# Third group's base blocks moved ahead of its last unit, half of the first two groups' blocks drained by ScalarE with x added by transfers

## The reference, cut to what matters

```python
ek = exp(min(k, 30)); ekv = ek * v                       # here k = v = fside, r = x
nf, df = forward scan of (ekv, ek) over T with a decay per channel and batch
nb, db = the same scan backward
euk = exp(min(u + k, 30))
y = sigmoid(x) * (nf + nb - ekv + euk * v) / max(df + db - ek + euk, 1e-8) * (0.8 + 0.2 * tf)
h = silu(y @ rw1.T + rb1)                                # 64 wide
logits = (h @ rw2.T + rb2)[:, :16] + gates               # the top 2 of 16, softmax: coeff
base = y @ W.T + bias                                    # 1024 x 1024
xa = y @ A.T                                             # 16 experts of rank 16
out = x + base + (xa * coeff) @ B
```

## Time and profile before

| What | Value |
|---|---|
| median of 3 runs | 682.68 us (680.84 to 684.97) |
| profiled execution | 681.2 us |
| span of its trace (first to last instruction) | 679.3 us |
| granted TensorE clock, mean over the span | 0.962 of full |
| TensorE matmul busy | 591.5 us (87%) |
| VectorE busy | 517.9 us (76%) |
| ScalarE busy | 360.0 us (53%) |
| GpSimd busy | 369.0 us (54%) |

### The profile page before, as it was taken

One profiled execution on the slowest core, in us unless ns is written; L12 is line 12 of the kernel. 1 busy time (PEld: TensorE's weight loads), 2 busy tenths in 40 slices (PEclk: granted clock), 3 DMA queues, 4 the chain that ended last, 5 costly groups with the idle time before them and its releaser, 6 DMA issues.

```text
span 679.3 us, 6881 instructions
## 1 busy us (share of the span) xinstructions
PE 591.5 (87%) x2546; PEld 477.2 (70%) x2546; DVE 517.9 (76%) x578; ACT 360.0 (53%) x428; POOL 369.0 (54%) x183
## 2 busy tenths in 40 slices
PE   0143698979999849699999999999999999999997
PEld 0132476758878627588888887888788887888886
DVE  7999999999999997999789996999699322021202
ACT  5778898855745665747635574567455221011100
POOL 1899998868768872856535854485457401000100
PEclk9976799989999968989999999999999999999999
DMA  5334477526747711244413442336222502040112
GB/s 194 123 93 151 147 237 239 169 65 140 175 120 140 201 63 62 78 141 159 151 47 108 154 157 77 109 109 202 77 84 73 154 1 74 20 154 2 30 63 78
DMA packets 33249, 78.45 MB, mean 115 GB/s; under 512 B 4736, under 2 KB 4928, under 8 KB 33216
## 3 DMA queue, kind: packets, MB, share of 16 engines
q1 hardware_dynamic: 30912, 73.82, 33.1%
q0 software_dynamic: 2304, 4.20, 4.2%
HBM read 57.03 MB, written 20.97 MB: 115 GB/s over the span
## 4 chain that ended last, share of the span: by engine, by line
PE 73%; DVE 13%; POOL 6%; ACT 4%; issue 3%; DMA 1%; SPq 0%; POOLq 0%; DVEq 0%; ACTq 0%
PE acc L940 23%; PE acc L942 22%; PE acc L941 22%; DVE mix L739 2%; PE acc L951 2%; DVE mix L730 2%; DVE mix L734 2%; PE acc L952 2%; DVE mix L760 2%; DVE eu L749 1%; PE acc L989 1%; DVE yr L766 1%; DMA xo<-w_base 1%; POOL wx_lo L652 1%; DVE kv L744 1%
## 5 line engine op out<-in xcount | busy, mean ns | idle before, releaser
L940 PE MATMUL acc<-y_hi,wa_hi 128*128 128x512 f32 x640 | 258.7, 404 | 61.9 <-POOL y_lo L639 51.0
L941 PE MATMUL acc<-y_lo,wa_hi 128*128 128x512 f32 x640 | 255.0, 398 | 0.0
L942 PE MATMUL acc<-y_hi,wa_lo 128*128 128x512 f32 x640 | 254.8, 398 | 0.0
L940 PEld LDWEIGHTS acc<-y_hi,wa_hi 128*128 128x128 f32 x640 | 123.7, 193 | 94.3 <-POOL y_lo L639 52.3
L942 PEld LDWEIGHTS acc<-y_hi,wa_lo 128*128 128x128 f32 x640 | 123.4, 193 | 26.7
L941 PEld LDWEIGHTS acc<-y_lo,wa_hi 128*128 128x128 f32 x640 | 123.7, 193 | 25.2
L629 POOL TENSOR_TENSOR mix<-mix,kv 128x1024 f32<-128x1024 f32 x31 | 74.3, 2396 | 88.6 <-DVE mix L718 88.6
L773 DVE SCALAR_TENSOR_TENSOR xo<-acc,bias_sb,xo 128x512 f32<-128x512 f32 x64 | 46.7, 736 | 74.3 <-PE acc L942 73.0
L639 POOL TENSOR_TENSOR y_lo<-yr,y_hi 128x1024 fp32r<-128x1024 f32 x31 | 75.8, 2445 | 36.0 <-ACT y_hi L401 36.0
L652 POOL TENSOR_TENSOR wx_lo<-xa,wx_hi 128x512 fp32r<-128x512 f32 x16 | 20.8, 1322 | 115.0 <-ACT wx_hi L478 115.0
L604 POOL TENSOR_TENSOR mix<-mix,kv 128x1024 f32<-128x1024 f32 x31 | 74.2, 2394 | 8.8 <-DVE mix L760 8.8
(11 more groups left out here) (103 smaller groups left out, 695.0 us busy)
## 6 DMA issues: line engine op xcount, KB each, us to landing
kv<-f_cm SPq DMA_DIRECT2D x32, 512.0 KB, 3.4
yr<-x_cm SPq DMA_DIRECT2D x32, 512.0 KB, 3.4
out<-xo SPq DMA_DIRECT2D x64, 256.0 KB, 3.3
xo<-x_cm SPq DMA_DIRECT2D x64, 256.0 KB, 3.7
out<-xo POOLq DMA_DIRECT2D x16, 256.0 KB, 6.5
xa<-w_base SPq DMA_DIRECT2D x5, 512.0 KB, 3.6
xo<-w_base SPq DMA_DIRECT2D x3, 512.0 KB, 5.9
xo<-w_router_a SPq DMA_DIRECT2D x2, 480.0 KB, 3.4
```

The costliest lines, as they stand in the source:

```text
L940: nc.tensor.matmul(out_ap, wh, yh, start=start, stop=False)
L941: nc.tensor.matmul(out_ap, wh, yl, start=False, stop=False)
L942: return nc.tensor.matmul(out_ap, wl, yh, start=False, stop=stop)
```

## The change

Five things are done in one edit.

1. Blocks j = 4 to 7 of groups 0 and 1 (8 of the 16) are no longer evacuated by VectorE. ScalarE does `drain`: it adds the bias and writes the block to an `xo` slot; no x is loaded for them. Four transfers issued by GpSimd (`add_x`, one for each j = 4 to 7, 128 channels by 1024 time steps, from `x_cm` to `out`) add x. `drain(e)` waits until the slot's last `add_out` has landed.
2. Group 2 on TensorE: `hid_sum` (three matmuls into 64 rows) takes the place of `hid`; base blocks 0 and 1 for units 0 to 6 are made before the last unit; `last_unit` takes the last unit's high half before its low half; base block 2 for units 0 to 6 stands before `turn`. ScalarE makes the sigmoid directly from the sum (`sigmoid_sum`), without `low_rows` and `hidden`.
3. Unit 15: `inverse` and `ratio` are made in two halves, the later half in time first (`ratio_late`). Unit 16's `p1` moves from GpSimd to VectorE.
4. Group 3's routing stands one step earlier (`first_step(3)` is 19 for 20), with base block 2 for three units before `turn` and three behind it; group 4 makes base block 0 for its first five units before it asks for the last three.
5. Places of evacuations, adds, x loads and routing pieces in the steps of groups 0 to 4 are moved, by tables.

```diff
-        evacs_at = {(CB + 2, AFTER_FWD): (0, 2), (CB + 2, AFTER_FWD_NUM): (2, 4), (CB + 2, AFTER_BWD_DEN): (4, 5),
+        evacs_at = {(CB + 2, AFTER_FWD): (0, 2), (CB + 2, AFTER_FWD_NUM): (2, 4), (CB + 5, AFTER_FWD_NUM): (8, 9),
+                    (CB + 5, AFTER_BWD_DEN): (9, 11), (CB + 5, AFTER_SUM): (11, 12),
...
+        drains_at = {(CB + 2, AFTER_INVERSE): (4, 6), (CB + 3, AFTER_HI): (6, 7), (CB + 3, AFTER_EXP_K): (7, 8),
+                     (CB + 5, AFTER_EXP_K): (12, 13), (CB + 5, AFTER_INVERSE): (13, 14), (CB + 6, AFTER_HI): (14, 15),
+                     (CB + 6, AFTER_EXP_K): (15, 16)}
+        x_adds_at = {(CB, AFTER_LO): (4, 5), (CB + 1, AFTER_GATE): (5, 7), (CB + 1, AFTER_LO): (7, 8)}
         adds_at = {(CB + 2, AFTER_LO): (0, 3), (CB + 3, AFTER_GATE): (3, 6), (CB + 4, AFTER_GATE): (6, 8),
-                   (CB + 5, AFTER_GATE): (8, 10), (CB + 5, AFTER_LO): (10, 13), (CB + 6, AFTER_GATE): (13, 16)}
+                   (CB + 6, AFTER_GATE): (8, 11), (CB + 6, AFTER_LO): (11, 14), (CB + 7, AFTER_GATE): (14, 16)}
...
+            def drain(e):
+                G, j = divmod(e, CB)
+                act.wait_ge(out_done, e + 1)
+                if e < XBUF:
+                    act.wait_ge(part_stored[(e - 2) % PBUF], 16 * (PARTS // PBUF))
+                else:
+                    act.wait_ge(out_added[e % XBUF], 16 * (e // XBUF))
+                nc.scalar.activation(xo[:, e % XBUF, :], acc[:, out_bank(G, j), :], ACT.Identity,
+                                     bias=bias_sb[:, j:j + 1]).then_inc(drained, 1)
...
+            def add_x(j):
+                pool.wait_ge(part_stored[j % PBUF], 16 * ((j + CB) // PBUF + 1))
+                nc.gpsimd.dma_start(out[j], x_cm[j], accum_op=ALU.add,
+                                    max_dma_last_dim=4 * T).then_inc(x_added[j - CB // 2], 16)
...
                 if g in HALVED:
                     nc.vector.tensor_tensor_scan(a[:, T - 2:N - 1:-1], decay(g, N - 1), a[:, T - 2:N - 1:-1], a[:, T - 1:T],
                                                  ALU.mult, ALU.add).then_inc(late_num_bwd, 1)
+                    ratio_late(g)
...
+            def last_unit(G, kc):
...
+                pe.wait_ge(late_hi_ready, 1)
+                nc.tensor.matmul(sums, wr[:, kc, 0:HID], yh, start=False, stop=False)
+                nc.tensor.matmul(sums, wr[:, kc, HID:2 * HID], yh, start=False, stop=False)
+                for a in range(2):
+                    nc.tensor.matmul(ranks[a], wa_hi[:, kc, cols[a]], yh, start=False, stop=False)
+                    nc.tensor.matmul(ranks[a], wa_lo[:, kc, cols[a]], yh, start=False, stop=False)
+                pe.wait_ge(late_lo_ready, 1)
+                nc.tensor.matmul(sums, wr[:, kc, 0:HID], yl, start=False, stop=True).then_inc(hid_done, 1)
...
+                elif G == SPLIT:
+                    bank_in(G, 0)
+                    made = 0
+                    for kc in range(CB - 1):
+                        while made < (kc if kc == CB - 2 else kc - LAG + 1):
+                            if made == 0:
+                                bank_in(G, 4)
+                            for j in range(2):
+                                base(G, j, made)
+                            made += 1
+                        unit_in(G, kc)
+                        hid_sum(G, kc)
...
+                    last_unit(G, CB - 1)
...
-                ahead = 4 if G == SPLIT else 0
+                ahead = {0: CB, SPLIT: CB - 1, 3: 3}.get(G, k0)
```

More of the change, by code:

```diff
@@ L211, in decay_mix_with_routed_lora_channel_major @@
         part_out = sem("part_out")
+        x_added = [sem(f"x_added{j}") for j in range(CB // 2)]
+        drained = sem("drained")
         out_added = [sem(f"out_added{i}") for i in range(XBUF)]
@@ L339, in _ @@
                 ended = ends_at.get(s, -1)
+                if 1 <= s < UNITS - 1 and ended in (SPLIT, SPLIT + 1):
+                    load_k(s + 1)
                 if ended >= 0:
@@ L344, in _ @@
                     store(G * CB)
-                if 1 <= s < UNITS - 1:
+                if 1 <= s < UNITS - 1 and ended not in (SPLIT, SPLIT + 1):
                     load_k(s + 1)
@@ L373, in _ @@
                     load_x(e)
+            for j in range(CB // 2):
+                sp.wait_ge(x_added[j], 16)
             for i in range(XBUF):
@@ L505, in _ @@
                 late_split, late_sigmoid = held(s - 1), held(s - 2)
-                third = s == first_step(SPLIT)
-                if q == 1 and G != SPLIT:
+                if s == THIRD:
+                    split_late_hi(s - 1)
+                    sigmoid_r(s)
+                    scale_end_den(s)
+                    sigmoid_sum(SPLIT)
+                    copy_xa(SPLIT)
+                    exps()
+                    split_hi(s - 1)
+                    scale_end_num(s)
+                    exp_gap(SPLIT)
+                    exp_uk(s)
+                    exp_k(s + 1)
+                    copy_turned(SPLIT)
+                    split_wx(SPLIT)
+                    inverse(s)
+                    continue
+                routed = q == 1 and G != SPLIT
+                if routed:
                     sigmoid_z(G)
@@ L561, in _ @@
                     exps()
[L562 removed]
+                if q == 0:
                     low_rows(G)
@@ L567, in _ @@
                     inverse(s)
-                if third:
-                    copy_turned(G)
+                drains(s, AFTER_INVERSE)
+                if routed and G == 1:
+                    split_wx(G)
                 for n in chunks_at(hi_steps, s):
@@ L678, in _ @@
                     split_lo(s - 1)
-                if q == 1 and G == SPLIT:
-                    split_wx(G)
+                if s == THIRD:
+                    split_wx(SPLIT)
+                for j in tiles(x_adds_at, s, AFTER_GATE):
+                    add_x(j)
                 for e in tiles(adds_at, s, AFTER_GATE):
@@ L856, in _, with groups_at @@
             link(nc.vector.tensor_copy(d_ps[:, 0:UNITS], d_g[:, :, :].rearrange("p b c -> p (b c)")))
-            def first_groups(s, place):
+            def groups_at(s, place):
                 for e in tiles(evacs_at, s, place):
                     evacuate(*divmod(e, CB))
+                if (s, place) in hidden_at:
+                    hidden(hidden_at[s, place])
+                if (s, place) in silu_at:
+                    silu(silu_at[s, place])
+                if (s, place) in routing_at:
+                    routing(routing_at[s, place])
+                if (s, place) in weigh_at:
+                    weigh(weigh_at[s, place])
             for s in range(STEPS):
                 G, q = quarter(s)
-                stored = q == 2 and G >= SPLIT
+                stored = q == 2 and G > 4
                 ended = ends_at.get(s, -1)
-                ending = ended >= 0
+                ending = ended > 4
                 if ending:
@@ L946, in y_of, with hid_sum @@
                 return y_hi[:, s, :], y_lo[:, s, :]
+            def hid_sum(G, kc):
+                yh, yl = y_of(G, kc)
+                three(acc[0:HID, banks[G][0], :], wr[:, kc, 0:HID], wr[:, kc, HID:2 * HID], yh, yl, kc == 0, False)
+            def last_unit(G, kc):
+                yh, yl = y_of(G, kc)
+                cols = [slice(a * P, (a + 1) * P) for a in range(2)]
+                sums = acc[0:HID, banks[G][0], :]
+                ranks = [acc[:, banks[G][1 + a], :] for a in range(2)]
+                pe.wait_ge(late_hi_ready, 1)
[6 more added lines that the diff above has]
+                nc.tensor.matmul(sums, wr[:, kc, 0:HID], yl, start=False, stop=True).then_inc(hid_done, 1)
+                for a in range(2):
+                    nc.tensor.matmul(ranks[a], wa_hi[:, kc, cols[a]], yl, start=False, stop=True).then_inc(xa_done, 1)
             def hid(G, kc):
@@ L1067, in _ @@
                             low_rank(G, a, kc)
+                    if G == 4:
+                        bank_in(G, 3)
+                        for kc in range(first):
+                            base(G, 0, kc)
                     for kc in range(first, CB):
@@ L1117, in _ @@
                 for j in range(3, 5):
-                    for kc in range(k0 + 2, k0 + 4):
+                    for kc in range(k0 + first, k0 + 4):
                         base(G, j, kc)
```

265 lines of the change are left out of this document (147 added, 118 removed).

## The result

The changed kernel takes 674.5 us (median of 4 runs, 673.5 to 675.1) against 682.4 us before (median of 4): ratio 0.9884, 95% interval 0.9858 to 0.9911, so 7.9 us are won. The forecast was 672.0, a gain of some 10. The profiled execution has a span of 672.4 us, 6.9 less than before.

What follows compares the result with a forecast made beforehand. TensorE's waits and low clock between 222.40 and 288.83, some 25 us, were the bound, with VectorE setting the time until unit 15. 18.4 won less 8.2 in group 4 is 10.2; 682.68 becomes 672.5, stated 672.0, range 664 to 680.

Steps and rivals of the forecast that it cites:

- the likeliest case: The forecast itself, rated against its rivals: 18.4 us won less 8.2 given back, time 669 to 675, chance 0.45.
- forward(13) waits for p1(13): VectorE, step 13: forward(13) can begin at 203.0 instead of 205.68, 2.7 won, with some 4 us of VectorE idle.
- at 222.4 again: TensorE: the order of groups 0 and 1 hardly changes, so group 2 begins at 222.4 as before.
- The drain waits for a landing: ScalarE near 224: drain of e = 14 waits 4 to 6 us for add_out(8), issued at 222.4, landing at 228.4.
- give nothing at this point: VectorE up to ratio(14): relief by ScalarE wins nothing, as 4 us won are lost waiting for a transfer.
- rival B: Adds land early enough or drain 14's wait hides; TensorE never waits for unit 15's high half: 665 to 669, chance 0.20.
- TensorE at unit 15: Group 2: TensorE waits 2.9 us for the high half at 249.1; group 3 begins at 300.8, 18.4 won.
- Group 4: TensorE waits 5.8 us for unit 23 and loses 2.4 in clock: 8.2 given back, 10.2 left.
- From `ratio(23)` to its low half are 8.5: Unit 23, asked for in group 4: low half ready 8.5 us after ratio(23), at z + 90.6, z being group 3's start.
- Each us there is one us at the end.: VectorE's steps 20 to 23: each us longer or shorter than counted moves the end by one us.
- Rival F: Slow x transfers delay add_out(0), so drain(6), ScalarE and VectorE wait: 20 slower, 700; decides from about 14 each; chance 0.06.
- between 2.33, after which the clock stayed up, and 3.64, after which it fell: TensorE, group 2: the 2.9 us wait lies between these; clock taken as up, 2 us kept for the other case.

Runs made afterwards that it cites:

- experiment 4: Changed kernel with weigh(3) behind three VectorE operations, the inverse of unit 20 ahead of the wx split on ScalarE, p1(21) ahead of it on GpSimd: 668.9 us, ratio 0.9804.
- experiment 5: Changed kernel with four edits together: early adds, load of r(24) ahead of two stores, p1(13) and p1(21) ahead of wx_lo, late weigh(3): 666.3 us, ratio 0.9768.
- experiment 6: Changed kernel with only two edits: p1 ahead of the low halves of wx in groups 1 and 3, and late weigh(3): 666.6 us, ratio 0.9769.
- experiment 11: Kernel with all four edits, plus five more base blocks moved ahead in group 4 and scale_end_den(12) ahead of the xa copies on ScalarE: 665.1 us, ratio 0.9738.
- Experiment 7: Changed kernel with part one undone: all 16 evacuations of groups 0 and 1 on VectorE, no ScalarE drains, no x adds in memory: 675.9 us, ratio 0.9905.
- Experiment 1: Changed kernel with the adds of e = 8 to 10 issued a step earlier, at the end of GpSimd's step 13: 671.9 us, ratio 0.9861.
- experiment 8: Changed kernel with TensorE's group 2 order undone for base block 1, its seven blocks again behind the last unit: 678.3 us, ratio 0.9940.
- Experiment 2: Changed kernel with the load of r(24) issued ahead of the stores of e = 30 and 31 in SP's queue: 673.0 us, ratio 0.9866.
- Experiment 9: Changed kernel with group 4's five advanced base blocks put back behind its last three units: 677.3 us, ratio 0.9926.
- experiment 12: Changed kernel without the four transfers that add x in main memory: 674.4 us, ratio 0.9885.

## Why the prediction was right, and where it was off

The time (674.5) lies in the likeliest case (669 to 675), 2.5 above the 672.0 named, and the mechanism is the forecast one: won in group 2, part given back in group 4, none lost later. Its steps:

- **forward(13) waits for p1(13).** Right in kind and size: 3.89 us for "some 4". Its time was wrong, 205.28 for 203.0. The step by which `weigh` still waits for TensorE, whose `spread` stands where it stood, so that `wx_lo` is ready when it was, failed: `routing(1)` stands behind `p2(12)` now, TensorE waits 2.40 for its result, and `wx_lo` starts at 200.35 instead of 197.91. From the logits of group 1 to its first weighted half TensorE needs 17.75 us, where it needed 13.61: 4.1 lost, 2.4 in this wait and some 1.6 in eight matmuls at the half clock behind it. So it begins group 2 at 224.85 and not "at 222.4 again"; the prediction had put this term at nothing. Where the clock stayed up behind the same wait (experiments 4, 5 and 6) it is 16.7. This was not undone alone; experiment 11, next to it, could not settle its worth.
- **The drain waits for a landing.** Right, but 2.90 us and not 4 to 6: the adds were issued at 224.80 (expected 222.4) and the first was there after 4.0, where 6.0 was taken. Two errors cancel by luck, and `ratio(14)` is at 235.06 for 234.5. Experiment 7 fits "give nothing at this point": all of part one is worth 1.4 by the median, which the intervals do not tell from nothing. What the prediction did not see is where this wait surfaces: drain 15 stands behind it, and TensorE waits 1.50 for its bank. Experiment 1 shows that this cost some 2, so rival B's mechanism was worth some 2 us, not the 4 it was given.
- **TensorE at unit 15.** Predicted 2.9 of waiting, none came. The high half ends at 250.65 and TensorE starts with it at 250.70: it had lost 1.50 and 2.40 before. Group 3 begins at 302.19 where 300.8 was forecast, 17.0 won instead of 18.4. That this is so near is partly luck: 2.4 and 1.5 of waiting at other places stand for the 2.9 that did not come. For a wait of 2.9 the prediction took the clock as up. It was not put to the test there, but behind 2.71 (experiment 4) and 2.60 (experiment 5) the clock fell, so this was not safe.
- **The 7 blocks ahead of the last unit** win part of these 17.0: experiment 8, 3.8 us by the median at the end and 4.6 at the logits of group 3, counted from the first weighted half of group 1. The rest of the 17.0 (unit 15 in two halves, group 2's routing and sigmoid, group 3's routing a step earlier, the moved evacuations) was not undone piece by piece, and its shares are not shown.
- **Group 4.** The term that was off most in the sum. Forecast 5.8 + 2.4 = 8.2, measured 7.46 and 2.7 for the clock, 10.4 from logits to logits. The 50.6 from `weigh(3)` to `ratio(23)` were right, 50.84. "From `ratio(23)` to its low half are 8.5" was not: 10.01, because the load of r(24) now stood in SP's queue behind the store of e = 31, whose evacuation the change had moved to the end of step 23. The prediction took its 8.5 from the trace before, where this load was issued 5.0 us ahead of `ratio(23)` (383.66 and 388.69), and did not follow what now stood ahead of it in SP's queue. Experiment 2 gives 8.47 and 5.90, the forecast's own numbers.
- **"Each us there is one us at the end."** Experiment 4 moved `ratio(23)` by 2.8 and got these 2.8, and another 2.2 through the load and the clock. Experiment 9 says the same from TensorE's side: 3.2 us more of waiting, 2.8 at the end.
- **x transfers cost nothing** that the intervals show (experiment 12) and **nothing lost at unit 31** (6.6 won at the logits of group 4, 6.9 at those of group 7): both right. Rival F needed 14 us for one transfer; they landed after 5.3 to 8.5 us.

## What to carry to other kernels

When work is moved into one engine's idle time, look next at the engine that it waits for: here VectorE was tied to TensorE by one operation (`weigh`) in the middle of its step, and the time won came back as a wait two groups later. The cheapest cure was to put independent work ahead of that operation. Follow every queue that an edit passes, loads behind stores too, and do not add up gains measured alone: four whose medians add up to 10.9 made 8.2 together, two of the four made the same, and the distances in the traces (15.4 against 8.1) say it more clearly. Compare traces by distances between two marks in the same trace, since what lies ahead of the edit moves by itself.

## What the runs showed of the hardware

- The granted clock can fall after a wait of TensorE, and not always at once. Behind 7.46 us 12 matmuls lay 0.43 apart (half clock), behind 5.90 only 8; behind 2.71 the first three distances were 0.34, 0.24 and 0.23, as at full clock, and only then came eight of 0.43. A shorter wait thus saved less clock than expected: 8 matmuls were lost behind 2.7 as behind 5.9.
- The length of the wait does not settle it. At the same place, with the same 2.33 us of waiting, the clock stayed up in the trace before and nine matmuls went at the half clock in experiment 1's. Behind 1.54 us at the logits of group 0 nine did in the trace after, and none in experiment 4's; behind 1.50 at 232.73 none did. Each such fall costs 8 to 9 matmuls 0.2 each, under 2 us, in one execution and not in another. From 80 us to the logits of group 1 experiment 1's trace has 31 matmuls at the half clock, the trace after 16, and those logits are 3.0 later. It is not the whole reason why they wander: experiment 6's trace has 11 and is still 1.8 later than the trace after. The prediction's "between 2.33, after which the clock stayed up, and 3.64, after which it fell" is therefore no bound. First experiment 1, then the trace after:

```profile
86.40:90.10 3.70, 3.68 (x9) 2.94 (x10) 3.21 (x3) 3.67 (x5) 3.70 (x2) 0.55 0.87 276
...
133.80:137.20 3.40, 3.40 (x9) 2.64 (x8) 3.14 (x22) 3.39 (x7) 3.24 (x3) 0.50 0.64 172
```

- Transfers that add in main memory: x from main memory, 512 KB, landed 5.3 to 8.5 us after their issue, median 7.4, and from SBUF, 256 KB, 4.0 to 7.7, median 6.1:

```profile
L746 POOL DMA_DIRECT2D out<-x_cm x4: 826/896/1116, 126.0 to 139.7; - x4
...
DMA to landing us min/median/max: 5.3/7.4/8.5
```

Twice the bytes took 1.3 us more by the medians, not twice the time. The sources differ too, and other transfers were under way, so this is what was seen in this kernel and not the price of the bytes.
